# A fused AdaLN block: one instruction program per engine, the first expert unit placed among the recurrence's last products

## The reference

```
h = layernorm(x) * (1 + ca) + sa
u = h @ W_in + b_in
gate_x = sigmoid(u @ W_gx + b_gx);  gate_a = sigmoid(u @ W_ga + b_ga)
a = exp(-8 * gate_a * softplus(a_param));  s = sqrt(1 - a*a)
state[t] = a[t] * state[t-1] + s[t] * gate_x[t] * u[t]
x = x + ga * (state @ W_out + b_out)

h = layernorm(x) * (1 + cb) + sb
probs = softmax(h @ gate_w)              # 8 experts
g, m = top_k(probs per expert, k = 512)  # each expert picks 512 of the sequence's 2048 tokens
y = gelu(h[m] @ w1[e]) @ w2[e]           # hidden width 1024
x = x + gb * bfloat16(scatter_add(g * y at m))
```

## Time and profile before

| | us |
|---|---|
| median of 3 runs | 1107.43 (1107.06 to 1108.64) |
| the profiled execution | 1107.6 |
| its span, first to last instruction | 1105.8 |
| PE busy with products | 1047.0 |
| ACT / DVE / POOL busy | 778.8 / 727.5 / 459.0 |
| mean granted TensorE clock | 0.973 |

### The profile page before, as it was taken

How to read it: one execution, slowest core, us unless ns; L and a number is a source line. 1 busy time by engine, 2 the same in 40 slices (tenths; PEclk the granted TensorE clock), 3 DMA queues, 4 the chain that set the end, 5 groups by cost and what they waited for, 6 DMA issues and landing times.

```text
span 1105.8 us, 18688 instructions
## 1 busy us (share of the span) xinstructions
PE 1047.0 (95%) x6922; PEld 924.7 (84%) x6922; DVE 727.5 (66%) x1680; ACT 778.8 (70%) x1236; POOL 459.0 (42%) x422
## 2 busy tenths in 40 slices
PE   7889999999749999999999999999999999999985
PEld 6778888888637888998899988899988899988875
DVE  4689989998758888975445645545545554447554
ACT  3668987887158887777677677776677776678751
POOL 2123432332314554455354454444554444544542
PEclk8999999999769999999999999999999999999998
DMA  7057755532256455456233435435245342355890
GB/s 253 4 130 196 237 142 134 116 70 61 67 50 184 119 125 160 118 139 145 44 54 83 117 71 118 83 92 138 43 116 112 84 111 39 61 128 144 268 338 39
DMA packets 96891, 130.85 MB, mean 118 GB/s; under 512 B 17312, under 2 KB 82464, under 8 KB 95776
## 3 DMA queue, kind: packets, MB, share of 16 engines
q1 hardware_dynamic: 62960, 84.11, 24.3%
q0 software_dynamic: 33024, 44.75, 23.1%
q10 hardware_dynamic: 816, 0.79, 0.2%
HBM read 78.96 MB, written 42.27 MB: 110 GB/s over the span
## 4 chain that ended last, share of the span: by engine, by line
PE 61%; DMA 3%; DVE 2%; ACT 2%; issue 2%; POOL 1%; SPq 0%; ACTq 0%; DVEq 0%; POOLq 0%
PE psum L1901 30%; PE psum L1878 28%; DMA w_raw<-ffn_rows 2%; PE psum L1854 2%; PE psum L420 1%; DMA out_x<-res_t 1%; DVE w L1700 1%; POOL ffn_rows L1547 0%; ACT hf L1670 0%; DMA ffn_rows<-rows_y,idx_cur 0%; ACT xf L1598 0%; ACT rows_in L1640 0%; ACT xT L1604 0%; ACT w L1633 0%; DVE xT L1743 0%
## 5 line engine op out<-in xcount | busy, mean ns | idle before, releaser
L1901 PE MATMUL psum<-xT,w 128*128 128x512 f32 x1536 | 374.3, 400 | 7.8 <-ACT hf L1670 7.5
L1878 PE MATMUL psum<-w,hidT 128*128 128x256 f32 x3072 | 364.3, 280 | 0.0
L1878 PEld LDWEIGHTS psum<-w,hidT 128*128 128x128 f32 x3072 | 357.9, 188 | 0.1
L1901 PEld LDWEIGHTS psum<-xT,w 128*128 128x128 f32 x1536 | 287.5, 191 | 68.7 <-ACT hf L1670 8.4
L1756 DVE TENSOR_TENSOR hidT<-hf,hidT 128x512 fp32r<-128x512 f32 x256 | 176.1, 692 | 226.4 <-ACT hidT L1674 226.0
L1547 POOL DMA_INDIRECT ffn_rows<-rows_y,idx_cur x120 | 211.9, 1765 | 223.0 <-issue 164.2
L440 POOL DMA_INDIRECT rows_in<-x_rows,idx_cur x128 | 136.3, 1065 | 175.7 <-DVE idx_cur L413 145.6
L1674 ACT ACTIVATE hidT<-hf 128x512 fp32r<-128x512 f32 x256 | 161.8, 632 | 8.1
L1670 ACT ACTIVATE hf<-psum 128x512 f32<-128x512 f32 x256 | 151.2, 591 | 16.1 <-PE psum L1901 5.5
L1614 ACT ACTIVATE rows_y<-psum,g_cur 128x256 f32<-128x256 f32 x124 | 51.9, 470 | 147.7 <-PE psum L1878 147.7
L1640 ACT ACTIVATE rows_in<-rows_in 128x256 f32<-128x256 f32 x128 | 66.4, 596 | 15.4 <-PEq L611 15.4
(11 more groups left out here) (205 smaller groups left out, 1220.7 us busy)
## 6 DMA issues: line engine op xcount, KB each, us to landing
w_raw<-in_L_ffn_w SPq DMA_DIRECT2D x30, 1024.0 KB, 5.7
x_rows<-x SPq DMA_DIRECT2D x16, 516.0 KB, 3.9
x_buf<-in_L_attn_x SPq DMA_DIRECT2D x16, 512.0 KB, 5.7
ffn_rows<-scratch SPq DMA_DIRECT2D x8, 1024.0 KB, 8.5
x_buf<-bias_bc POOLq DMA_DIRECT2D x16, 512.0 KB, 6.8
scratch<-x_rows SPq DMA_DIRECT2D x12, 512.0 KB, 10.4
out_x<-scratch SPq DMA_DIRECT2D x12, 512.0 KB, 8.7
w_raw<-ffn_rows SPq DMA_DIRECT2D x12, 512.0 KB, 8.0
```

Source lines behind the costliest of these rows:

```text
L1878: ins = pe.matmul(y_tile(u, t), hidT[qs][:, k, t * P:(t + 1) * P], w2_s[n % 2][qm][:, k, :], start=(x_ == 0), stop=(x_ == len(terms) - 1))
L1901: ins = pe.matmul(H_bank[m % 4], w1_s[n % 2][qs][:, k, m * P:(m + 1) * P], xT[qm][:, k, :], start=(x_ == 0), stop=(x_ == len(terms) - 1))
```

## The change

The two blocks become one: every engine has one program, with no meeting point between the halves. What the barrier had ensured is taken over by single waits (`r_x1s`, `s_zero`, `q_pz`, `r_b`, `s_ga`). The buffers of the second half are laid over those of the first, with spacers, in an order in which early ones lie on dead ones. Then work moves:

- Low and high quarters 0 and 1 of load 0 are made in step 8 of the recurrence: on ACT behind that step's last instruction, on DVE ahead of `keep_turned`. Load 1's `w1` is issued in step 10.
- In the drain, list 0 is made ahead of `residual(14)` and `scan(15)`, `fetch(0)` stands ahead of `rstd2(14)`, unit 0's rows are transposed ahead of `project(15)`, and `turn_x1(15)`, `score(15)`, `make_list(2)` stand inside `layer1(0)`.
- Unit 0 has two H banks in place of four, as `psT` and the others are still used.
- Unit 0 has no rounds, unit 5 has six; `ties` moves from behind block 2 to behind block 5 of unit 5. `exp_scores(act, 1)` (softmax of sequences 1 to 3) moves from the second block's beginning to behind the GELUs of unit 0, `store_probs(sp, 1)` from the front of SP's second block to behind the load of `w2` of load 1.

```diff
+                    if s == PAIR_AT + 2:
+                        sp.wait_ge(f_ws, 2)
+                        sp.dma_start(w1_raw[:], w1_v[LOADS[1]]).then_inc(f_w1, 16)
...
                 for n in range(1, NL):
-                    sp.wait_ge(f_ws, 4 * (n - 1) + 2)
-                    sp.dma_start(w1_raw[:], w1_v[LOADS[n]]).then_inc(f_w1, 16)
+                    if n >= 2:
+                        sp.wait_ge(f_ws, 4 * (n - 1) + 2)
+                        sp.dma_start(w1_raw[:], w1_v[LOADS[n]]).then_inc(f_w1, 16)
                     sp.wait_ge(f_ws, 4 * (n - 1) + 4)
                     sp.dma_start(w2_raw[:], w2_v[LOADS[n]]).then_inc(f_w2, 16)
+                    if n == 1:
+                        store_probs(sp, 1)
...
+                    if d == NG - 2:
+                        fetch(pool, 0)
                     if d is not None:
                         rstd2(d)
...
-                    if s == NG + 2:
-                        fetch(pool, 0)
                 fetch(pool, 1)
...
-                        act.activation(warm[:], quarter[:], ACT.Tanh if c_ + 1 < NG else ACT.Exp)
+                        act.activation(warm[:], quarter[:], ACT.Tanh if c_ + 1 < NG else ACT.Gelu_apprx_tanh)
+                    if s == PAIR_AT:
+                        for q in range(2):
+                            split_hi(0, q)
+
+                keep_x1T(NG - 3)
+                for q in range(2, 4):
+                    split_hi(0, q)
+                keep_x1T(NG - 2)
+                normalise(0)
...
+                    for m in range(KH):
+                        if u == 0 and m == 2:
+                            keep_x1T(NG - 1)
+                        if u == 0 and m == 6:
+                            normalise(1)
...
+                    if u == 0:
+                        exp_scores(act, 1)
+                        for n, q in work[2:]:
+                            split_hi(n, q)
...
                     if s == PAIR_AT:
+                        for q in range(2):
+                            split_lo(0, q)
                         chosen.keep_turned()
...
-                gated_u(NG - 1)
+                chosen.keep_slots()
+                slots_of(dve, 0)
+                for half in range(2):
+                    places_of(dve, 0, half)
+                scaled_u(NG - 1)
+                keep_list(dve, 0)
+                gated_input(NG - 1)
+                keep_scores(NG - 3)
+                residual(NG - 2)
                 scan(NG - 1)
-                chosen.keep_slots()
-                residual(NG - 2)
-                list_first(dve, 0)
-                keep_scores(NG - 3)
+                slots_of(dve, 1)
+                for half in range(2):
+                    places_of(dve, 1, half)
+                split_lo(0, 2)
+                rows_lo(0)
+                keep_gates(0)
                 residual(NG - 1)
-                list_first(dve, 1)
+                keep_list(dve, 1)
                 keep_scores(NG - 2)
-                keep_scores(NG - 1)
+                for m in range(KH):
+                    lo(0, m)
+                    if m == 1:
+                        split_lo(0, 3)
+                    if m == 2:
+                        slots_of(dve, 2)
+                    if m == 3:
+                        places_of(dve, 2, 0)
+                    if m == 4:
+                        keep_scores(NG - 1)
+                        places_of(dve, 2, 1)
+                    if m == 5:
+                        dve.wait_ge(s_zero, 16 * ZEROS)
+                        dve.wait_ge(q_pz[0], 16)
+                        dve.wait_ge(r_se, NG)
+                        chosen_later.shift()
+                    if m == 7:
+                        keep_list(dve, 2)
+                chosen_later.share()
+                for q in range(2):
+                    split_lo(1, q)
+                for u in range(1, NU):
...
+                        if u == 0 and m == 2:
+                            turn_x1(NG - 1)
+                        if u == 0 and m == 4:
+                            score(NG - 1)
+                        if u == 0 and m == 6:
+                            pe.wait_ge(r_sr, NG)
+                        if v and m == (6 if u == 0 else 5 if late else 2):
+                            make_list(pe, v)
...
+                        if u == 1 and t == 0:
+                            pe.wait_ge(f_xf, 2)
+                            turn_probs(pe, 1)
...
                 turn_x1(NG - 3)
+                turn_slots(pe, 0)
                 project(NG - 2)
-                turn_slots(pe, 0)
                 score(NG - 3)
+                make_list(pe, 0)
+                turn_x1(NG - 2)
+                score(NG - 2)
+                turn(0)
                 project(NG - 1)
-                turn_x1(NG - 2)
-                make_list(pe, 0)
-                score(NG - 2)
-                turn_x1(NG - 1)
                 make_list(pe, 1)
-                score(NG - 1)
```

More of the change, by code:

```diff
@@ L437, in fetch @@
                 pool.wait_ge(q_pz[1], 16 * len(LATER))
+                for n in range(2):
+                    pool.wait_ge(r_x1s[n], 16 * (NG // 2))
             pool.sem_inc(held[0], 1)
@@ new lines, in adaln_kernel, with quarter_of @@
+        acc16 += [sbf(f"acc16_{n}", [P, TT, D], BF16) for n in range(2, GB)]
+        def quarter_of(w_s, q):
+            raw, parts, half = (w1_raw, w1_s[w_s], q) if q < 2 else (w2_raw, w2_s[w_s], q - 2)
+            return raw, parts, slice(half, half + 1) if q < 2 else slice(half * KH // 2, (half + 1) * KH // 2)
+        f_w1 = sem("w1_loaded")
+        f_w2 = sem("w2_loaded")
+        f_wh = sem("weights_hi_copied")
+        f_ws = sem("weights_split")
+        f_n = sem("rows_normalised")
@@ new lines, in adaln_kernel, with acc_of, res_of @@
+        res_t = ([scratch[:, n * TT * D:(n + 1) * TT * D].rearrange("p (t d) -> p t d", d=D) for n in range(4)]
+                 + res_own)
+        SA, SR = len(acc_t), len(res_t)
+        def acc_of(k):
+            return res_t[2 + k % 2] if k < GB else acc_t[k % SA]
+        def res_of(k):
+            return res_t[k % 2] if k < GB else res_t[k % SR]
+        EARLY_LOAD = 10
+        assert LAST_OF[EARLY_LOAD - 3] + 1 >= DONE_IN[0] + 3 and EARLY_LOAD + GB <= NL - 1
+        AHEAD_A, AHEAD_R = SA, SR - 1
@@ L611, in adaln_kernel, with rounds_until, rounds_of @@
+        def rounds_until(u):
+            return sum(PER_UNIT[:u])
+        def rounds_of(u):
+            if u >= CHOSEN_IN:
+                return [None] * 6
+            here = [rounds_until(u) + j for j in range(PER_UNIT[u])]
+            return here + [None] * (6 - len(here))
+        moe.close()
         with nc.Block() as block:
@@ new lines, in _ @@
+                for k in range(GB):
+                    sp.wait_ge(o_out[k], 16)
+                sp.wait_ge(f_ws, 4 * NL)
+                for k in range(GB, GB + AHEAD_R):
+                    load_x1(k)
+                for k in range(GB, GB + AHEAD_A):
+                    load_acc(k)
+                for k in range(GB, NG):
+                    store(k)
+                    if k + AHEAD_A < NG:
+                        load_acc(k + AHEAD_A)
+                    if k + AHEAD_R < NG:
+                        load_x1(k + AHEAD_R)
@@ L670, in _ @@
+                for n in range(SR):
+                    sp.wait_ge(o_out[n], 16 * len(range(n, NG, SR)))
             @block.gpsimd
@@ L751, in _ @@
+                for u in range(NU):
+                    if u >= 1 and u + 1 < NU:
+                        fetch(pool, u + 1)
+                    if u >= 1 and u - 1 not in DIRECT:
+                        add(u - 1)
+                    if u in DIRECT:
+                        fetch_sums(u)
+                for u in DIRECT:
+                    store_direct(u)
+                pool.wait_ge(f_out, 16 * CT * 2)
             @block.scalar
@@ new lines, in weigh @@
+                def weigh(u, half):
+                    if half == 0:
+                        act.wait_ge(f_g, u + 1)
+                        if u >= 2:
+                            act.wait_ge(f_add[UNITS[u - 2][1]], 16 * CT * (turn_of(u - 2) + 1))
+                    act.wait_ge(f_Y, 2 * u + half + 1)
+                    for t in range(half * CT // 2, (half + 1) * CT // 2):
+                        ins = act.activation(rows_y[u % 2][:, t, :], y_tile(u, t), ACT.Copy, scale=g_cur[u % 2][:, t, 0:1])
+                    ins.then_inc(f_y, 1)
@@ L842, in _, with normalise @@
+                def normalise(u):
+                    act.wait_ge(f_in[u % 2], 16 * CT * (u // 2 + 1))
+                    x_u = rows_in[u % 2]
+                    for t in range(CT):
+                        ins = act.activation(x_u[:, t, 0:D], x_u[:, t, 0:D], ACT.Identity, bias=x_u[:, t, D:D + 1],
+                                             scale=x_u[:, t, D + 1:D + 2])
+                    ins.then_inc(f_n, 1)
+                for s in range(1, NG + 1):
                     a, c_, _, _, e_ = stages(s)
```

(2 more changed lines are left out.)

919 lines of the change are left out of this document (428 added, 491 removed).

## The result

| | before | after |
|---|---|---|
| median of the runs beside each other, us | 1107.82 (1107.06 to 1108.64) | 1118.2 (1117.73 to 1119.66) |
| ratio to before, 95% interval | | 1.0093 [1.008, 1.0107] |
| span of the profiled execution, us | 1105.8 | 1116.9 |
| predicted, us | | 1111.0 (1100 to 1115.5) |

The change makes the kernel 10.4 us slower. The direction was forecast as the likelier one, the size was not: the time lies above the range.

What follows compares the result with a forecast made beforehand. From 350 us on the time was taken as PE's own, so gains lay only in the passage between the halves. 1107.6 + 8.7 - 22.5 + 4.8 + 10.6 + 1.7 = 1110.9, so 1111 us, range 1100 to 1115.5.

Steps and rivals of the forecast that it cites:

- term 1: Recurrence, steps 8 and 9: PE waits for the weight splits before step 9, then runs at low clock; +8.7 us.
- term 2: Start of unit 0: earlier lists and gather bring the first hidden product forward; -22.5 us, bounds -24 and -19.
- term 3: Within unit 0: moved score work and waits for places and lists lengthen it; +4.8 us, bounds +3 and +8.
- term 4: Unit 1: w1 of load 2 lands late behind the probabilities' store, PE waits for hits; +10.6 us, bounds +1.3 and +12.
- term 5: Unit 5: two more rounds, and ties delaying the low parts that PE waits for; +1.7 us.
- at nothing, other addresses: Whole kernel: moving buffers to other addresses costs nothing, as no row shows an effect; 0 +/- 1.
- the bound of -19: Start of unit 0: smallest gain allowed there, if project(15) also runs at half clock; -19 us.
- w1 isn't held up: Unit 1: w1 of load 2 lands in the usual 5.0 us despite the store; 1101.6 us, chance 0.15.
- The step-9 stall is given back: Recurrence: the stall before step 9 doesn't hold or later slack absorbs it; about 1103 us, chance 0.08.
- Smaller stalls: Stalls smaller than worked out: w1 lands near 332, or one clock drop doesn't come; 1107 us, chance 0.2.
- The clock stays down: Unit 0: PE's clock stays low, its first 12 products taking 4.7 not 3.0; 1114 us and over, chance 0.13.
- The change doesn't do what it says: Drain: the gather isn't earlier, unit 0 starts near 310 while the stalls stay; 1118 us, chance 0.03.

Runs made afterwards that it cites:

- the last kernel: The changed kernel with five edits (store later, quarters spread, weight residues restored, keep_list(2) earlier, unit 5's last low quarter later), plus rows_in on multiples of 64: 1097.86 us.

## Why the prediction was right in direction and too small

Sum of the stretches: predicted +8.7 - 22.5 + 4.8 + 10.6 + 1.7 = +3.3; measured 11.1 between the spans. The missing 7.8 by step (rounding adds 0.1):

| | predicted | measured | miss |
|---|---|---|---|
| term 1, step 8 and 9 | +8.7 | +7.4 | -1.3 |
| term 2, start of unit 0 | -22.5 | -20.8 | +1.7 |
| term 3, within unit 0 | +4.8 | +7.1 | +2.3 |
| term 4, unit 1 | +10.6 | +11.7 | +1.1 |
| term 5, unit 5 | +1.7 | +1.8 | +0.1 |
| at nothing, other addresses | 0 | +4.0 | +4.0 |

**The step that failed is "Other addresses: no row shows an effect; 0 +/- 1".** The trace of before did show one: from turn(7) on its units take 23.74 and 23.28 us in turn, in a loop whose iterations do the same work and wait for nothing. I had read PE as saturated from 350 us on and stopped there, so I never asked what its pace depends on. Two neighbouring units differ in the buffers they use; a change that moves nearly every buffer may then have a price that is not zero. None of the rivals had it. The kernel before with other weight addresses and the kernel after with the old ones give it from both sides, 4.7 and 4.1 us in the medians. With 4.0 for this term the sum is 1114.9, inside the range; the other 3.8 of the miss are in the terms below.

**Term 1** stood as a mechanism: wait 6.0 predicted, 6.10 measured, and it vanishes when only the place of the splits is changed. The clock's part was too large: 2.7 predicted, 1.6 measured (1.94 + 1.69 for two sets of transposes against 1.03 + 1.04; the projection behind them runs at 3.62, full pace). The step that failed there is to charge a gap of any length what the gap in the drain had cost. There the clock was 0.50 from 284.6 to 291.3, and 5.3 us of that were work; here it was 0.50 for about as long, from 152.2 to 158.8, but over half of it passed in the gap itself, and 3 us were left. Only what was left when the work resumed cost time. Of the 8.3 that step 9's projection was late, 0.9 came back by step 16.

**Term 2**: lists and gather moved as worked out, the first hidden product came at 308.49, against "near 308". The step mis-sized is project(15), taken at full clock (3.3 to the next product) and measured at 4.5, its row at 4.66: part of the case that stood as the bound of -19, since at the half clock throughout it takes 6.46. PE also waited 1.00 for the normalised rows at 301.84. It was the gap of 3.28 ahead of 294.17 that took the clock down; it was 0.50 up to 305.6.

**Term 3**: the waits were 1.01 and 0.80 ahead of the list and 2.75 ahead of turn(1), 4.6 in all against 4.0 predicted. What I had left out is that such waits take the clock down here too, though I had charged just that in terms 1 and 4. It fell twice. Behind the first two waits blocks 6 and 7 took 4.59 and not 3.01 (granted clock 0.50 from 322.9 to 326.1): 1.6. Behind the third turn(1) took 1.80 and not 1.03, the first tile of products 3.98 and not 2.87: 1.9. With the 0.6 of the waits that is 4.1 us, almost twice the miss; by luck "the remainder keeps its length" was wrong as well. Before had a wait of 2.14 us for hits in that stretch, which is gone in after:

```profile
344.10 0.16 PE L293 MATMUL psum<-n_hit,same_e 128*128 128x3 bf16 x1 [2.14 <-DVE hit L217]
```

**Term 4**: the mechanism was exact and the two parts missed in opposite ways: a wait of 10.09 for 7.8, the clock 1.6 (4.64 against 3.01) for 2.7. The wait was longer by 2.3 because `w1` left 1.7 after its buffer was free, and landed in 13.8, not 13.2. The buffer was free when forecast, by the clock of unit 1: 9.3 us ahead of its first product (334.37 and 343.70), where the forecast had 9.4 (323.0 and 332.4). But SP was then still issuing the store, which I had left out. The store's descriptors thus cost twice, on SP and on the DMA engines. The clock's part was small for the reason of term 1: it fell 6.5 us ahead of the end of the wait (0.50 from 353.6 on) and was back at 363.8.

**Term 5** came out in both parts: from turn(5) to turn(6) after takes 0.48 longer than before (0.4 predicted for two more rounds), from turn(6) to turn(7) 1.19 (1.3 predicted for the wait on `hidT`, which is 1.03). Part of it may be the slower pace, since weight buffer 1 is already in use there (the kernel before with other addresses is 0.4 behind between turn(2) and turn(7)).

**The rivals.** *w1 isn't held up* fell: 13.8 with the store ahead of it, 5.7 without. The Trainium skill, DMA: Bandwidth & Descriptors, "Queues, rings and completion order", has one issuer's descriptors consumed in ring order on each DMA engine; the trace agrees, by the same 13.8 and 5.7. *The step-9 stall is given back* fell but for 0.9: +7.4 still at step 16. *Smaller stalls* was right for the clock's share alone. *The clock stays down*: its deciding sign didn't come (unit 0's first 12 products took 3.01), but it fell again later in unit 0. *The change doesn't do what it says* gave about the right time, 1118, for a wrong reason: the gather did come early, at 292.33. The drain of about 1.38 us that the Trainium skill (ScalarE: Activation LUTs, "What ACT_TABLE_LOAD costs") adds to each table load is not in this trace: the instruction before ends at 353.32 + 2.07 = 355.39, the load takes 355.41 to 356.69 and GELU 0 begins at 356.70. There the trace decides.

What the clock costs was read from rows at either level; no run tried it alone.

## What to carry to other kernels

Before taking a saturated loop as fixed, compare its iterations: if they do the same work in different time, suspect the buffers' addresses, and keep each buffer's residue when the layout changes, or charge for it. When a transfer is moved in a queue, look at what it is now ahead of: 6,000 small packets kept the issuer busy for 4 us, 1.7 of which the next transfer waited, and made that transfer land 8 us later; the engine at the end of the chain waited 8.8 us more. What a wait costs beside its length is the low clock that is left behind it: ask it of every new wait, not of the long ones alone. An early piece of work belongs behind what others wait for in its step: two splits in front of one copy of 0.28 us cost 7 us, and spread over two steps nothing.

## What the runs showed of the hardware that was not expected

- **Pace of products and the address of the weights.** The same 128x256 products of `w` and `hidT` take 276, 279 or 281 ns, with no wait. With weight buffer 1 at residue 1408 mod 2048 the loop from unit 7 on takes 4 us longer than with both buffers alike (626.6 against 622.2). A shift by 2048 bytes of all that follows `rows_in` changes nothing (1107.26 us).
- **The place of `rows_in` counts too, but not alone.** The pair 23.74/23.28 turns to 23.74 throughout by moving `rows_in1` alone, and to 23.28/23.74 by moving both and the list buffers. Units in which PE reads the same buffers can still run at either pace (23.28 from turn(8), 23.74 from turn(10) in the last kernel). The cause is open.
- **The clock falls within the gap, and a gap's length doesn't tell its price.** After a gap of 2.67 us 5.3 us of work ran at the lower clock, after one of 6.10 only 3, because the rest of the low stretch lay in the gap. Behind waits of 0.80 and 1.01 us it fell (0.50 from 322.9 to 326.1), while in before it stayed at 1.00 behind the one of 2.14 us (341 to 345).
